# FFN of a Flamingo-style block: the normalised x as two float32r parts instead of three bf16 parts

## What is computed

```python
x = x + tanh(g_xattn[0]) * attention_map(layernorm(x), ctx)      # softmax(q k^T) of ctx
x = x + tanh(g_ffn[0])   * ffn(layernorm(x))                     # the part that changes
x = x + tanh(g_xattn[1]) * ssm(ctx, z=layernorm(x))              # state-space scan over ctx
x = x + tanh(g_ffn[1])   * moe(layernorm(x))                     # 64 experts, top 8
```

```python
gate, up = split(x @ ternary(w_gate_up).T)       # 256 -> 2 x 1024
h = silu(gate) * up
y = rms_norm(h) @ ternary(w_proj).T              # 1024 -> 256
```

## Time and profile before

| | us |
|---|---|
| median of three runs | 402.34 |
| lowest and highest run | 401.85, 402.37 |
| the profiled execution | 402.55 |
| its span, first to last instruction | 400.8 |
| TensorE matmuls busy | 336.8 (84%) |
| VectorE busy | 303.3 (76%) |
| ScalarE busy | 259.5 (65%) |
| GpSimd busy | 251.6 (63%) |

### The profile page before, as it was taken

One profiled execution on the slowest core, in us unless ns is written; L12 is line 12 of the kernel. 1 busy time (PEld: TensorE's weight loads), 2 busy tenths in 40 slices (PEclk: granted clock), 3 DMA queues, 4 the chain that ended last, 5 costly groups with the idle time before them and its releaser, 6 DMA issues.

```text
span 400.8 us, 6924 instructions
## 1 busy us (share of the span) xinstructions
PE 336.8 (84%) x1910; PEld 264.6 (66%) x1921; DVE 303.3 (76%) x669; ACT 259.5 (65%) x532; POOL 251.6 (63%) x198
## 2 busy tenths in 40 slices
PE   3957974698799689979896179999999999999994
PEld 2342653365567466656786168888888888888873
DVE  2999999799999999999899955545554544555476
ACT  1698999899888898897273535445445544554422
POOL 4200025879997796797522487878878787887510
PEclk9996895799999999999999559999999999999999
DMA  8940620767435887432098447888888888864455
GB/s 230 368 149 0 172 82 24 239 202 241 151 113 163 259 266 257 159 137 74 18 260 197 132 112 170 221 226 236 217 213 226 220 227 233 229 162 92 65 160 177
DMA packets 57834, 70.96 MB, mean 177 GB/s; under 512 B 6658, under 2 KB 42162, under 8 KB 57810
## 3 DMA queue, kind: packets, MB, share of 16 engines
q1 hardware_dynamic: 49104, 56.04, 46.3%
q0 software_dynamic: 7536, 14.56, 15.8%
q10 hardware_dynamic: 1170, 0.08, 0.2%
HBM read 61.75 MB, written 8.91 MB: 176 GB/s over the span
## 4 chain that ended last, share of the span: by engine, by line
PE 43%; DVE 13%; ACT 11%; issue 6%; DMA 5%; POOL 3%; DVEq 0%; SPq 0%; POOLq 0%
PE bank L1344 14%; PE bank L1367 11%; PE bank L1337 7%; PE bank L1324 4%; DVE bank L1583 4%; DMA ssm<-bc_rows 3%; ACT ssm L874 3%; ACT L912 2%; DVE ssm L1588 2%; ACT L874 2%; POOL ssm L617 2%; PE bank L1330 2%; PE bank L1178 2%; DMA B_last<-bc_rows 1%; ACT ffn L912 1%
## 5 line engine op out<-in xcount | busy, mean ns | idle before, releaser
L617 POOL TENSOR_TENSOR ssm<-ssm,arena 128x1024 f32<-128x1024 f32 x31 | 73.1, 2359 | 17.8 <-issue 13.0
L1588 DVE TENSOR_TENSOR_SCAN ssm<-ssm,bank 128x512 f32<-128x512 f32 x64 | 78.1, 1221 | 4.5 <-issue 2.2
L690 POOL DMA_INDIRECT ssm<-routed,idx x64 | 67.7, 1058 | 21.8 <-issue 18.3
L1344 PE MATMUL bank<-places,ye_parts 128*128 128x512 f32 x264 | 75.8, 412 | 0.5 <-DVE ye_parts L1800 0.5
L1808 DVE SCALAR_TENSOR_TENSOR ssm<-ssm,bank 128x96 f32<-128x96 f32 x64 | 20.1, 314 | 73.2 <-ACT ssm L986 73.2
L701 POOL DMA_INDIRECT sums<-ssm,idx x31 | 53.2, 1716 | 15.1 <-issue 9.1
L986 ACT ACTIVATE ssm<-bank 128x96 f32<-128x96 f32 x64 | 16.1, 251 | 70.5 <-PE bank L1367 70.5
L1367 PE MATMUL bank<-arena,ssm 128*128 (+1 forms) x256 | 54.0, 333 | 1.0 <-ACT ssm L969 1.0
L1178 PE MATMUL bank<-xs,wguT 128*128 128x512 bf16 x182 | 43.5, 387 | 12.3 <-POOL xs L604 6.3
L1344 PEld LDWEIGHTS bank<-places,ye_parts 128*128 128x128 f32 x264 | 45.4, 189 | 12.1 <-DVE ye_parts L1800 0.9
L1367 PEld LDWEIGHTS bank<-arena,ssm 128*128 128x128 f32 x256 | 45.7, 194 | 7.2 <-issue 1.6
(11 more groups left out here) (227 smaller groups left out, 663.9 us busy)
## 6 DMA issues: line engine op xcount, KB each, us to landing
ssm<-bc_rows SPq DMA_DIRECT2D x22, 512.0 KB, 3.8
arena<-bc_rows SPq DMA_DIRECT2D x16, 512.0 KB, 5.2
arena<-in_L_ffn_gate_proj SPq DMA_DIRECT2D x32, 192.0 KB
arena<-in_L_ffn_up_proj SPq DMA_DIRECT2D x32, 192.0 KB
arena<-in_L_ffn_down_proj SPq DMA_DIRECT2D x32, 192.0 KB
B_last<-bc_rows SPq DMA_DIRECT2D x10, 512.0 KB, 3.8
sums<-zero_f SPq DMA_DIRECT2D x1, 2304.0 KB, 14.0
arena<-in_L_ffn_w_gate_up SPq DMA_DIRECT2D x1, 2048.0 KB, 11.2
```

What stands on the lines that cost most here:

```text
L617: pool.tensor_tensor(prod[:, a:b, :], hs[:, a:b, :], C_all[:, 2 * (q % 8):2 * (q % 8) + 2, :], ALU.mult).then_inc(s.prod_ok, 1)
L690: pool.indirect_dma_start(out=xe[:, k, :], out_offset=None, in_=routed, in_offset=bass.IndirectOffsetOnAxis(ap=idx2[:, k, 0:1], axis=0)).t ...
L1344: ins = pe.matmul(bank[4 + 2 * h + t][:, :], ye_parts[:, b, c, h * P:h * P + P], places[:, b, 4 * t:4 * t + 4, :], start=False, stop=False ...
L1588: dve.tensor_tensor_scan(hs[:, k % 4, :], dA[:, k % 3, :], x[:, :], 0.0, ALU.mult, ALU.add).then_inc(s.scan_ok, 1)
```

## The change

The normalised x becomes two float32r parts, `x_high` and `x_low`, and the gate and up weights become float32r tiles `w_gate` and `w_up`. `x_high` and the start of `w_up` take the place of the three bf16 parts, the rest of `w_up` lies over the transposed ctx, which is no longer needed then, `x_low` lies where the float32 rest was, and `w_gate` where the bf16 weights were. `keep_middle` and `rest_low` go, with their semaphores. A unit has 8 gate and up matmuls. `decay(5)` moves ahead of the SiLU of unit 0.

```diff
+        w_gate = nc.alloc_sbuf_tensor_at("w_gate", [P, 2, H], F32R, offset=at_wgu).ap()
+        w_up = nc.alloc_sbuf_tensor_at("w_up", [P, 2, H], F32R, offset=at_xs + 2 * TOK * 4).ap()
+        x_high = nc.alloc_sbuf_tensor_at("x_high", [P, 2, TOK], F32R, offset=at_xs).ap()
+        x_low = nc.alloc_sbuf_tensor_at("x_low", [P, 2, TOK], F32R, offset=at_xnT).ap()
...
-            def rest_low(k):
-
-                kc, c = k % 2, slice((k // 2) * 512, (k // 2) * 512 + 512)
-                pool.wait_ge(s.xs_mid, k + 1)
-                pool.tensor_tensor(xs[:, 2, kc, c], xnT[:, kc, c], xs[:, 1, kc, c], ALU.subtract).then_inc(s.xs_lo, 1)
-
-            rest_low(0)
-            rest_low(1)
...
-                if f in (1, 2):
-                    rest_low(f + 1)
...
-                dst = part(wguT[:, 0, 0:1], (2 * H, 2), (P, 4), (1, P), offset=k * 4 * P)
+                dst = part((w_gate, w_up)[k // 2][:, 0, 0:1], (H, 2), (P, 4), (1, P), offset=(k % 2) * 4 * P)
                 act.activation(dst, src, ACT.Copy).then_inc(s.quantT_sb, 1)
...
-                act.activation(xs[:, 0, kc, c], bank[1 + k][:, :], ACT.Copy).then_inc(s.xs_hi, 1)
-
-            def keep_middle(k):
-
-                kc, c = k % 2, slice((k // 2) * 512, (k // 2) * 512 + 512)
-                act.wait_ge(s.xs_rest, k + 1)
-                act.activation(xs[:, 1, kc, c], xnT[:, kc, c], ACT.Copy).then_inc(s.xs_mid, 1)
+                act.activation(x_high[:, kc, c], bank[1 + k][:, :], ACT.Copy).then_inc(s.xs_hi, 1)
...
             decay(0)
             decay(1)
-            keep_middle(0)
-            keep_middle(1)
             keep_quantised(2)
             keep_quantised(3)
...
                     decay(4)
+                    decay(5)
...
-                if 4 * f + 5 < STEPS:
+                if f > 0 and 4 * f + 5 < STEPS:
                     decay(4 * f + 5)
...
-                if f < 2:
-                    keep_middle(f + 2)
...
-                        for part3 in range(3):
-                            ins = pe.matmul(bank[(7, 0)[g]][:, :], wguT[:, kc, hc * P + g * H:hc * P + g * H + P],
-                                            xs[:, part3, kc, th * 512:th * 512 + 512], start=n == 0, stop=n == 5)
+                        for values in (x_high, x_low):
+                            ins = pe.matmul(bank[(7, 0)[g]][:, :], (w_gate, w_up)[g][:, kc, hc * P:hc * P + P],
+                                            values[:, kc, th * 512:th * 512 + 512], start=n == 0, stop=n == 3)
                             n += 1
...
-                if f % 8 == 0:
-                    pe.wait_ge(s.xs_lo, 2 + 2 * (f // 8))
                 gate_up(f)
...
-                dve.tensor_tensor(xnT[:, kc, c], bank[1 + k][:, :], xs[:, 0, kc, c], ALU.subtract).then_inc(s.xs_rest, 1)
+                dve.tensor_tensor(x_low[:, kc, c], bank[1 + k][:, :], x_high[:, kc, c], ALU.subtract).then_inc(s.xs_rest, 1)
```

More of the change, by code:

```diff
@@ L129, in __init__ @@
         self.xs_rest = sem("xs_rest")
-        self.xs_lo = sem("xs_lo")
         self.scan_ok = sem("scan_ok")
@@ L205, in __init__ @@
         self.q_step = sem("q_step")
-        self.xs_mid = sem("xs_mid")
         self.coef_ok = sem("coef_ok")
@@ L233, in build @@
         xw = sb("xw", [P, NT, XW])
+        at_xnT = nc.sbuf_base
         xnT = sb("xnT", [P, 2, TOK])
+        at_xs = nc.sbuf_base
         xs = sb("xs", [P, 3, 2, TOK], BF16)
```

## The result

The changed kernel is faster: median 399.50 us (398.69 to 399.68), beside 402.36 for the kernel before in the same comparison, a ratio of 0.9908 (0.9879 to 0.9937). Two later comparisons gave 399.97 us, 0.9925 (0.9897 to 0.9953), and 398.94 us, 0.9898 (0.9859 to 0.9937); the median of all 17 runs is 399.53. About one run in five of the kernel before (23 of 113) took 404.48 to 406.94 us, mostly at a mean granted clock near 0.926, and none of the 17 of the changed kernel took over 401.62, but no such run was profiled, so its cause and its share in the ratios stay open. The predicted 400.1 us had the right place and too small a size: its one term, 2.2 us, is 2.8 on average over the profiled executions.

What follows compares the result with a forecast made beforehand. VectorE's steps were taken to bound the scan stage. Profiled 402.55 us less the 2.2 us hole gave 400.35, and with the median 0.2 below the profiled run 400.1 us (399.7 to 400.6, wider range 399.3 to 401.5).

Steps and rivals of the forecast that it cites:

- What bounds the stage: Scan stage, 67.9 to 196.9 us: VectorE's steps bound it; only two holes, 2.2 and 0.8 us, and its start can be won.
- The chain behind the first hole: State 5's scan: ScalarE's middle parts, GpSimd's low parts, late cold gate matmuls, late SiLU, late decay(5), VectorE idle 2.23 us.
- The price of the hole: VectorE's idleness ahead of state 5's scan, 80.08 against 77.88 us: closing it gains 2.2 us, the sum's only term.
- Its wider range: Whole kernel: 399.3 to 401.5 us, taking in the forecast and the rivals of a smaller and a larger gain.
- a larger gain: Rival, chance 0.08: the hole near the stage's end goes too, 3.0 us gained in all, 399.3 us.
- State 8 as the tightest place: State 8's scan in the stage: decay(8) ends at 83.9 us, wanted at 84.05, 0.15 us of slack.
- The shorter bursts: Gate and up matmuls, 8 per unit for 12: 0.7 us less per unit on TensorE, costed at nothing beside VectorE's steps.
- float32r writes at nothing: ScalarE's keep_high and keep_quantised writing four bytes instead of two: no added time, 1.3 us on ScalarE as upper bound.
- The second hole stays: Stage's end: VectorE's 0.8 us wait of hidden(15) for the last SiLU, behind its table load and the last decay, remains.
- The smaller gain: Rival, chance 0.14: the hole moves to state 8 or another wait opens, costing 0.6 to 1.2 us; 400.7 to 401.3 us.
- single cold units: Units of the stage at half clock: TensorE 2.8 us late, hidden by the SiLU's some 2 us of slack when alone.
- the slower rival: Rival, chance 0.08: the clock falls in the scan stage; three cold units in a row cost 6.4 us, 406.5 us.

Runs made afterwards that it cites:

- e9: Changed kernel with two 128x512 copies put back on ScalarE ahead of keep_quantised(2), nothing reading what they write; 400.58 us, ratio 0.9935 to the kernel before.
- e5: Changed kernel with twelve float32r gate and up matmuls per unit, the low part multiplied twice; 400.08 us, ratio 0.9932 to the kernel before.
- e7: Changed kernel with the last SiLU and its table load ahead of the last decay, decay(63); 399.19 us, ratio 0.9917 to the kernel before.
- e16: Changed kernel, unchanged, run again; 398.94 us, ratio 0.9898 to the kernel before.
- e3: Kernel before with only decay(5) moved ahead of the first SiLU, old data types kept; 403.14 us, ratio 0.9993 to the kernel before.
- e4: Changed kernel with decay(5) put back behind the first SiLU, so the data types alone; 400.26 us, ratio 0.9926 to the kernel before.
- e14: Kernel before, unchanged, profiled once more for the size of the hole at state 5; 402.65 us.
- e8: e7 with twelve transposes of the identity at the kernel's start as a warm start; 399.86 us, ratio 0.9932 to the kernel before.
- e10: e9 with two 128x512 subtractions also put back on GpSimd, for which gate_up(0) waits; 400.60 us, ratio 0.9943 to the kernel before.
- e13: Kernel before with five matmuls of zeros in TensorE's idle time ahead of gate_up(0); 402.52 us, ratio 0.9983 to the kernel before.
- e17: The same kernel as e7, run beside e16 on the same chip; 398.78 us, ratio 0.9892 to the kernel before.

## Why the prediction was right, and where it was short

**What bounds the stage**: right. The stage less VectorE's waits is 124.4 to 124.7 us in every row of the table, with four matmuls or twelve, with the old data types or the new.

**The chain behind the first hole**: right, link by link. The copies gave 1.04 us on ScalarE as worked out (e9: 67.82 to 68.86 again). State 5's scan was forecast near 77.9 without idleness; with the stage 0.56 earlier it came at 77.32. `gate_up(0)` started at 69.4, 1 us ahead of the 70.4 forecast: the stage was 0.56 early, and TensorE started 0.14 us after the last copy and not 0.5. The half microsecond was read from an incomplete row, in which `gate_up(0)` has 11 records for 12 matmuls. TensorE's weight loads in the timeline of before show that the first record is the one missing:

```profile
72.66 0.14 PEld L1178 LDWEIGHTS bank<-xs,wguT 128*128 128x128 bf16 x2 [6.17 <-issue]
73.07 0.15 PEld L1178 LDWEIGHTS bank<-xs,wguT 128*128 128x128 bf16 x1 [0.28 <-issue]
```

TensorE began near 72.7, some 0.15 us after GpSimd's last subtraction ended at 72.54.

**The price of the hole, 80.08 - 77.88 = 2.2 us, the only term of the sum: this is the step that failed.** It was read from one execution as if it were a property of the kernel. In three of six it is 3.4 us, since `gate_up(0)` then runs at 1.2 GHz to its end. The stage of before is 128.27 us on average, that of the changed kernel 125.47, a gain of 2.80. From the 402.34 of the first three runs that gives 399.54, where the 17 runs have 399.53, but so close a fit is luck: from the 402.71 of all runs it gives 399.9. The profiled spans, 400.97 and 397.70 on average, differ by 3.27 us, of which 0.17 lie ahead of the stage and 0.30 behind it, assigned to nothing here. The prediction had both facts beside each other, the "late and cold gate matmuls" and the SiLU that waited for them, and did not ask what the wait would be without the rise of the clock: 1.1 us more. Its wider range, from 399.3, takes in 399.5 only by the rival of a larger gain, whose mechanism did not come: that is luck.

**State 8 as the tightest place, with 0.15 us of slack**: right. `decay(8)` began at 82.54 and, at 0.71 us, ended 0.2 ahead of the scan at 83.45; 1.04 us taken away in e9 gave a wait of 0.77 there and nowhere else.

**The shorter bursts at nothing**: right to 0.4 us (e5). **float32r writes at nothing**: right; the groups of ScalarE after are those of before to 1%:

```profile
L831 ACT ACTIVATE x_high<-bank 128x512 fp32r<-128x512 f32 x4 | 2.1, 583 | 0.0
...
L824 ACT ACTIVATE w_up<-bank 128x1024 fp32r<-128x1024 bf16 x2 | 1.9, 1037 | 0.0
L824 ACT ACTIVATE w_gate<-bank 128x1024 fp32r<-128x1024 bf16 x2 | 1.9, 1026 | 0.0
```

**The second hole stays, and by ScalarE's order**: right; e7 removes it by that order alone.

**The rivals.** The larger gain came to the right time by the wrong way: it wanted the second hole gone. The smaller gain's price is that of e9. The clock did fall in the stage, which the first profile of before never showed; TensorE in windows of the changed kernel:

```profile
107.00:112.00 5.00, 5.00 (x19) 0.66 0.47 162
138.00:142.00 4.00, 4.00 (x15) 0.57 0.84 287
169.50:173.50 4.00, 4.00 (x16) 0.61 0.47 152
```

No VectorE wait lies in or behind any of them. The Trainium skill's advice on gaps ("TensorE: Matmul & The Clock Gate", section "Why this matters for your kernels") agrees with this trace on the level and not on the time: TensorE was idle for 2.80 to 2.82 us ahead of each fall, and its slack, some 2 us in a unit, swallowed each, as the prediction said of single cold units. Idleness does not tell it all: the level held in the first profile of before after 2.17 us (to 172.09), and fell in e16 after 1.04 (to 145.75). Nor is the fall the change's alone: with twelve bf16 matmuls the level fell once or twice in four of the six profiles of before, and in e3.

Not every fall was free. In e16 the level fell at 146 us; ScalarE and VectorE behind it:

```profile
151.65 0.60 ACT L898 ACTIVATE ffn<-bank 128x512 f32<-128x512 f32 x1 [2.12 <-PE bank L1162]
...
154.36 1.22 DVE L1570 TENSOR_TENSOR_SCAN ssm<-ssm,bank 128x512 f32<-128x512 f32 x1 [0.17 <-DVE bank L1565]
```

The SiLU waited 2.12 us for gate matmuls, and VectorE 0.17 for the decay behind that SiLU; e4 has the same pair, and e14, of the kernel before, 1.07 and 0.21. So the mechanism of the slower rival exists and costs 0.2 us here: 2.12 - 0.17 = 1.95 us of slack bears out the prediction's 2, while e14, with a copy of up behind that SiLU, had 0.86.

## What to carry to other kernels

A wait that ends with a matmul burst begun after idleness has no single price: ask which clock level the burst had in the profile, and price the wait at the other level too, or profile several executions before pricing it. Measure a local change by the length of its stage, which repeated to 0.25 us wherever the clock took the same course in the first burst, and not by the span, whose other parts moved by up to 2 us here. When a hole on the bounding engine closes, look at once for what its next instruction now overlaps: 0.8 of 0.96 us went to GpSimd at the stage's end.

## What the runs showed of the hardware

The same 128x1024 product on VectorE took 1.23, 1.58 and 2.38 us with 0, 0.51 and 1.30 us of a GpSimd product beside it. At the kernel's start the granted clock reads 1.00 while four float32 matmuls (eight records) took 5.1 to 6.7 us that took 3.70 in e8, after twelve transposes: the granted clock does not show this slowness. ScalarE waited for the landing of the gate and up weights near 16 us in six of the 20 profiles (2.08 us in e3, 2.05 in e8, 0.17 to 0.96 in e5, e10, e13 and e17), and the start of the stage then hangs on it.
